# In the last two blocks VectorE instead of ScalarE makes every second high half of the turned probabilities

## The chip, the cores and the metric

The kernel runs on one core of one Trainium2 chip. The metric is the device time of one execution in microseconds (us); shorter is better. Before the change it is 729.9 us, the median of 3 runs (729.87 to 730.22).

## The reference, cut to what matters

The layer that this case touches is an attention over a graph with 4096 nodes: scores, a mask by the adjacency matrix, a softmax along each row, and the weighted mean of `value`.

```python
def _L1_gnn_ref(x, neigh, adj, ...):
    neib_att = jnp.tanh(neigh @ Wn1 + bn1) @ Wn2 + bn2
    value = neigh @ Wv + bv
    x_att = jnp.tanh(x @ Wx1 + bx1) @ Wx2 + bx2
    ws = jnp.einsum('nh,mh->nm', x_att, neib_att)
    ws = jax.nn.leaky_relu(ws, negative_slope=0.01)
    ws = jnp.where(adj > 0, ws, jnp.float32(NEG_BIG))
    ws = jax.nn.softmax(ws, axis=1)
    agg_neib = ws @ value
    return jnp.concatenate([x @ Wfx + bfx, agg_neib], axis=1)
x = _layernorm(x + _L0_gnn_ref(x, adj, ...))
x = _layernorm(x + _L1_gnn_ref(x, neigh, adj, ...))
```

`_L0_gnn_ref` averages the neighbours' rows (mask @ x over the degree) and mixes them with the node's own row through small weight matrices.

## The kernel before, in words

The 4096 rows are worked on in 32 blocks of 128 rows (b = 0 to 31). Along the 4096 neighbours a block has 8 chunks of 512 columns. All engines walk through the same numbered slots s; `due(s, at)` gives the block and the chunk whose turn it is, so that chunk k of a step with the offset `at` comes up in slot 8b + k + at. Several blocks are in work at the same time: in slot 8b + 23 + k the scores of chunk k are made (`SCORE_AT`), in slot 8b + 31 the row maximum (`ROW_MAX_AT`), then four exponentials of 1024 columns in the order quarter 1, 0, 2, 3 in the slots 8b + 32, 33, 34 and 36 (`EXPS`). The order within a slot is that of each engine's loop over s, and every engine works strictly in that order; semaphores carry the dependences.

The probabilities must stand transposed for the product with `value`. The first quarter (two chunks) goes over DMA: ScalarE rounds it to a high half (`wide_high`, L925), VectorE makes the low half, the rest that the rounding left (`wide_low`, L761), SyncE issues the DMA transposes (L376). The other six chunks are turned by TensorE; they are counted j = 0 to 5 here, and n = 6b + j over all blocks. One of them goes like this:

- TensorE transposes it into one of two PSUM buffers `ps_t[n % 2]` (`turn_p`, L1116, slot 8b + 33 + j). It waits for the exponential, and for the low half of turn n - 2.
- ScalarE copies it as f16 to `p_hi[:, n % 2]` (`p_high`, L920). It waits for the turn and, for the buffer, until weighing n - 2 has finished.
- VectorE subtracts: `p_lo = ps_t - p_hi` (`p_low`, L756). It waits for `p_hi_made`.
- TensorE multiplies both halves with the values (`weigh_values`, L1137, one slot later, 12 matmuls). It waits for the low half. The first weighing of a block also waits until VectorE has read the sums of the block before (`layer1`, L773).

In the slots in which block b's chunks are turned, block b + 1's scores are made: TensorE `scores` (L1107, two PSUM buffers), ScalarE `leaky` (L907), VectorE `masked_scores` (L692), and after its eighth chunk VectorE's `row_max` (L698, L701), which lets the exponentials (L913) of block b + 1 start. Block 31 has no block after it. Within a slot VectorE's order is `layer1`, `masked_scores`, `row_max`, `wide_low`, `p_low`; ScalarE's is `exps`, `wide_high`, `p_high`, `leaky`, `normalise2` (L937); TensorE's is `turn_p`, `scores`, `weigh_values`. GpSimd's `norm2` (L473 to L477) stands between `layer1` and `normalise2`, and the store of a block follows that.

Of the kernel before, what the change touches and what calls it, by code (L numbers as in the profile page):

```python
# [18 lines left out]
NB = N // P  # L19
# [5 lines left out]
NG = N // GW  # L25
# [22 lines left out]
NT = NB // TR  # L48
MASK_BUFS = 4
RES_BUFS = 4  # L50

# [18 lines left out]
TURN_AT = 33  # L72
# [6 lines left out]
BY_PE = NG - 2 * BY_DMA  # L79
# [16 lines left out]
def due(s, at, k=None):  # L96

    b, g = divmod(s - at, NG)
    return (b, g) if 0 <= b < NB and (k is None or g == k) else None
# [8 lines left out]
def turned_by_pe(s, at):  # L108

    d = due(s, at)  # L110
    return (*d, d[0] * BY_PE + d[1]) if d and d[1] < BY_PE else None


def at_least(eng, sem, value):
    if value > 0:
        eng.wait_ge(sem, value)


def gnn_kernel(nc, x, adj, w_self, b_self, w_nb, b_nb, w_comb, b_comb, neigh, wx1, bx1, wx2, bx2,
# [5 lines left out]
    with ExitStack() as ctx:  # L125
# [3 lines left out]
        def sem(name):  # L129
            return ctx.enter_context(nc.semaphore(name))  # L130
# [38 lines left out]
        p_hi, p_lo = p_both[:, 0], p_both[:, 1]  # L169
        res = late[:, 1024:2048].rearrange("p (r d) -> p r d", r=RES_BUFS)  # L170

# [53 lines left out]
        ps_t = [ctx.enter_context(nc.psum_tensor(f"ps_t{k}", [P, GW], F32)) for k in range(2)]  # L225
# [54 lines left out]
        pt_done = sem("pt_done")  # L280
        pv_done = sem("pv_done")
# [22 lines left out]
        m_split = sem("m_split")  # L304
        m_scaled = sem("m_scaled")
        p_hi_made = sem("p_hi_made")
        wide_hi_made = [sem(f"wide_hi_made{w}") for w in range(BY_DMA)]
        wide_lo_made = [sem(f"wide_lo_made{w}") for w in range(BY_DMA)]
        wide_t_in = [sem(f"wide_t_in{w}") for w in range(BY_DMA)]
# [119 lines left out]
        def _(pool):  # L429
# [35 lines left out]
            def add_biases(b):  # L465
                pool.wait_ge(x1_made, b + 1)
                at_least(pool, out_made, b - RES_BUFS + 1)
                pool.tensor_tensor(res[:, b % RES_BUFS, :], x1[:, :], bfv_sb[:, :], ALU.add).then_inc(resx_made, 1)  # L468

# [18 lines left out]
        def _(dve):  # L488
# [260 lines left out]
            def add_fx(b):  # L749
                dve.wait_ge(resx_made, b + 1)  # L750
                dve.scalar_tensor_tensor(out=res[:, b % RES_BUFS, 0:DV], in0=ps_x[:, 3 * P:4 * P], scalar=fx_inv,
                                         in1=res[:, b % RES_BUFS, 0:DV], op0=ALU.mult, op1=ALU.add).then_inc(res_made, 1)

            def p_low(b, j, n):
                dve.wait_ge(p_hi_made, n + 1)
                dve.tensor_tensor(p_lo[:, n % 2, :], ps_t[n % 2][:, :], p_hi[:, n % 2, :],  # L756
                                  ALU.subtract).then_inc(p_lo_made, 1)

# [5 lines left out]
            def layer1(b):  # L764
                base = 5 * b
                right = res[:, b % RES_BUFS, DV:D]
                dve.wait_ge(pv_done, NG * (b + 1))
# [44 lines left out]
        def _(act):  # L812
# [61 lines left out]
            def first_part(s):  # L874
                if s == 0:
                    n_high(PRE - 1)
                if (t := turn_due(s, 0)) is not None:
                    if t + 1 < NT:
                        copy_rows_t(t + 1)
                    v_high(t)  # L880
                if (t := turn_due(s, 1)) is not None:
                    hidden(t)
                if (t := turn_due(s, 2)) is not None:
                    n_high(t)
                if s + 2 < NT:
                    x_high(s + 2)
                if s in (6, 7):
                    act.wait_ge(m_scaled, 1)
                    act.activation(m16[:, 0, s - 6, :], m_both[:, s - 6, :], ACT.Copy, scale=m_scale).then_inc(m_hi_made, 1)

            def mean_of(b):
                act.wait_ge(degree_step, 2 * (b + 1))
                at_least(act, mean_t_done, b)
                act.activation(mean[:, :], ps_agg[b % 2][:, 0:D], ACT.Copy, scale=row[:, 5:6]).then_inc(mean_made, 1)

            def mean_high(b):
                act.wait_ge(mean_t_done, b + 1)
                at_least(act, combined, b)
                act.activation(mean_t[:, 0, :], ps_agg[b % 2][:, 0:D], ACT.Copy, scale=x_scale).then_inc(mean_hi_made, 1)

            def leaky(b, k):
                act.wait_ge(s_done, NG * b + k + 1)
                if k < 2 * BY_DMA:
                    at_least(act, wide_lo_made[k // 2], b - 1)
                else:
                    at_least(act, pt_done, BY_PE * (b - 2) + k - 2 * BY_DMA + 1)
                act.activation(score[:, b % 2, k * GW:(k + 1) * GW], ps_s[k % 2][:, :], ACT.Prelu, alpha=SLOPE,  # L907
                               scale=score_scale).then_inc(leaky_made, 1)

            def exps(b, q):  # L910
                act.wait_ge(max_step, 2 * (b + 1))
                part = score[:, b % 2, q * QW:(q + 1) * QW]
                act.activation(part, part, ACT.Exp, bias=exp_bias[:, b % 2:b % 2 + 1],  # L913
                               scale=score_unit).then_inc(exp_made, 1)

            def p_high(b, j, n):
                act.wait_ge(pt_done, n + 1)

                at_least(act, pv_done, NG * b + j - 1 if j >= 2 else NG * (b - 1) + BY_PE + j - 1)
                act.copy(p_hi[:, n % 2, :], ps_t[n % 2][:, :]).then_inc(p_hi_made, 1)  # L920

            def wide_high(b, w):
                act.wait_ge(exp_made, NQ * b + EXP_PLACE[w] + 1)
                at_least(act, wide_t_in[w], 32 * b)
                act.copy(wide_p[:, w, 0, :], score[:, b % 2, w * QW:(w + 1) * QW]).then_inc(wide_hi_made[w], 1)  # L925

            def normalise1(b):
                act.wait_ge(norm1_step, 3 * (b + 1))
                at_least(act, x1_t_done, b)
                at_least(act, resx_made, b)  # L930
                act.activation(x1[:, :], l0[:, :], ACT.Identity, scale=mv1[:, 3:4],  # L931
                               bias=mv1[:, 4:5]).then_inc(x1_made, 1)

            def normalise2(b):
                act.wait_ge(norm2_step, 3 * (b + 1))
                at_least(act, out_sent[b % 2], 16 * (b // 2))
                act.activation(out_sb[:, b % 2, :], res[:, b % RES_BUFS, :], ACT.Identity, scale=mv2[:, 3:4],  # L937
                               bias=mv2[:, 4:5]).then_inc(out_made, 1)

            def x1_high(b):  # L940
                act.wait_ge(x1_t_done, b + 1)
                at_least(act, hf_done, b)
                act.activation(x1_t[:, 0, :], ps_x[:, 0:D], ACT.Copy, scale=X1_SCALE).then_inc(x1_hi_made, 1)

            def x_tanh(b):
                act.wait_ge(hf_done, b + 1)
                at_least(act, xatt_done, b)
                at_least(act, tanh_split, b)
                for out in (tanh32, tanh16):
                    act.activation(out[:, :], ps_x[0:H3, 2 * P:3 * P], ACT.Tanh, bias=bx1_sb[0:H3, 0:1],  # L950
                                   scale=h1_inv[0:H3, :]).then_inc(tanh_made, 1)

            def xatt_high(b):
                act.wait_ge(xatt_done, b + 1)
                at_least(act, s_done, NG * (b - 1))
                act.activation(stack[:, b % 2, :], ps_x[0:H3, 0:P], ACT.Identity,
                               bias=bx2_sb[0:H3, 0:1]).then_inc(xatt_hi, 1)

            for s in range(0, SLOTS + 3):
                first_part(s)  # L960
                if d := due(s, MEAN_SPLIT_AT, 0):
                    mean_high(d[0])
                if d := due(s, X1_AT, 0):
                    normalise1(d[0])
                if d := due(s, X1_COPY_AT, 0):
                    x1_high(d[0])
                if d := due(s, TANH_AT, 0):
                    x_tanh(d[0])
                if d := due(s, STACK_AT, 0):
                    xatt_high(d[0])  # L970
                for at, q in EXPS:
                    if d := due(s, ROW_MAX_AT + 1 + at, 0):
                        exps(d[0], q)
                for w, at in enumerate(WIDE_HIGH_AT):
                    if d := due(s, at, 0):
                        wide_high(d[0], w)
                if d := turned_by_pe(s, TURN_AT):
                    p_high(*d)
                if d := due(s, SCORE_AT):
                    leaky(*d)  # L980
                if d := due(s, MEAN_AT, 0):
                    mean_of(d[0])
                if d := due(s, LAYER1_AT + 1, 0):
                    normalise2(d[0])
# [248 lines left out]
```

## Time and profile before

| | before |
|---|---|
| median of 3 runs | 729.9 us (729.87 to 730.22) |
| the profiled execution, its own time | 730.62 us |
| its span in the profile | 728.8 us |
| TensorE (PE) busy | 689.6 us, 95% |
| VectorE (DVE) busy | 621.7 us, 85% |
| ScalarE (ACT) busy | 573.5 us, 79% |
| GpSimd (POOL) busy | 129.9 us, 18% |

The shares are means over the whole span. The change touches only the last two blocks, whose turns lie in the last 35 us or so, and there the shares are others; so the trace has to be read by stretch and in order of time. Times in the rows are counted from the start of the span.

### The profile page before, as it was taken

The numbers are of one execution on the slowest core, as the hardware profiler recorded it, in microseconds if no ns is written. First come the engines' busy times: TensorE is split into PE (matmuls) and PEld (weight loads), VectorE is DVE, ScalarE is ACT, GpSimd is POOL, SyncE is SP. The second block draws the span as 40 slices with busy tenths as digits, with TensorE's granted clock in tenths as the row PEclk, the third lists the DMA queues.
The fourth block names the chain that finished last, engine by engine and source line by source line (L and its number), as shares of the span: only waits on it lengthen the run. The fifth ranks groups of instructions, "written<-read, shape, count | busy, mean of one in ns | idle before, by whom it ended". The sixth has DMA issues, their size and how long they took to land.

```text
span 728.8 us, 19763 instructions
## 1 busy us (share of the span) xinstructions
PE 689.6 (95%) x7344; PEld 592.1 (81%) x7344; DVE 621.7 (85%) x1535; ACT 573.5 (79%) x920; POOL 129.9 (18%) x242
## 2 busy tenths in 40 slices
PE   5989998999999999999999999999999999998775
PEld 4646676888888888888888888888888888886554
DVE  4887668999999999999999999999999999987874
ACT  2455248888888888888888888888888888889884
POOL 0010111222211222221111222211122221111101
PEclk9989999999999999999999999999999999999999
DMA  8967999999999999999999999999999999841111
GB/s 266 370 150 165 228 269 236 195 203 223 196 202 206 223 208 202 216 224 213 220 212 208 208 203 219 188 221 205 206 200 217 212 220 217 167 81 33 39 42 44
DMA packets 260145, 141.39 MB, mean 194 GB/s; under 512 B 225361, under 2 KB 243665, under 8 KB 260049
## 3 DMA queue, kind: packets, MB, share of 16 engines
q1 hardware_dynamic: 259604, 140.10, 88.7%
q8 instruction: 59, 0.97, 0.6%
q14 instruction: 38, 0.30, 0.1%
q10 hardware_dynamic: 444, 0.02, 0.0%
HBM read 81.35 MB, written 4.19 MB: 117 GB/s over the span
## 4 chain that ended last, share of the span: by engine, by line
PE 86%; ACT 5%; DVE 4%; issue 3%; POOL 1%; DMA 1%; SPq 0%; POOLq 0%; ACTq 0%
PE ps_v L1137 22%; PE ps_agg L1092 15%; PE ps_agg L1095 14%; PE ps_t L1116 10%; PE ps_s L1107 7%; PE ps_agg L1156 3%; PE ps_agg L1159 3%; PE ps_s L1006 2%; PE ps_v L1014 2%; PE ps_x L1176 1%; PE ps_x L1179 1%; ACT score L913 1%; PE ps_t L997 1%; PE ps_x L1023 1%; DMA neigh_sb<-in_L_gnn_neigh_dram 1%
## 5 line engine op out<-in xcount | busy, mean ns | idle before, releaser
L1092 PE MATMUL ps_agg<-x,mask_t 128*128 128x257 f16 x1024 | 243.4, 274 | 0.2 <-DMA mask_t<-mask 0.2
L1095 PE MATMUL ps_agg<-x,mask_t 128*128 128x256 f16 x1024 | 237.4, 273 | 0.3 <-DVE x L533 0.3
L907 ACT ACTIVATE score<-ps_s,sc 128x512 f32<-128x512 f32 x256 | 178.7, 698 | 63.1 <-PE ps_s L1107 57.6
L692 DVE CUSTOM_DVE_ANT_0 score<-score,mask 128x512 f32<-128x512 f32 x256 | 175.9, 687 | 16.7 <-ACT score L907 14.3
L1137 PEld LDWEIGHTS ps_v<-v,late 128*128 128x128 f16 x2304 | 143.9, 97 | 41.7 <-DVE late L756 16.9
L1137 PE MATMUL ps_v<-v,late 128*128 128x129 f16 (+1 forms) x2304 | 162.6, 219 | 11.6 <-DVE late L773 6.0
L913 ACT ACTIVATE score<-score,exp_bias,sc 128x1024 f32<-128x1024 f32 x128 | 159.4, 1246 | 3.2 <-DVE exp_bias L701 3.2
L756 DVE TENSOR_TENSOR late<-ps_t,late 128x512 f16<-128x512 f32 x192 | 130.7, 681 | 33.2 <-ACT late L920 31.4
L920 ACT CAST late<-ps_t 128x512 f16<-128x512 f32 x192 | 114.8, 598 | 20.4 <-PE ps_t L1116 20.4
L1116 PE MATMUL ps_t<-ident,score 128*128 128x128 f32 x768 | 116.8, 275 | 5.3 <-ACT score L913 5.1
L1095 PEld LDWEIGHTS ps_agg<-x,mask_t 128*128 128x128 fp8e4 x1024 | 100.3, 98 | 15.5 <-issue 5.2
L1092 PEld LDWEIGHTS ps_agg<-x,mask_t 128*128 128x128 fp8e4 x1024 | 100.5, 98 | 15.1 <-issue 0.8
L1107 PE MATMUL ps_s<-n,stack 96*128 96x512 f16 x256 | 97.3, 380 | 1.0 <-DVE stack L746 0.9
L544 DVE TENSOR_SCALAR mask<-adj_sb 128x1024 bf16<-128x1024 int32 x128 | 89.8, 704 | 3.9
L1116 PEld LDWEIGHTS ps_t<-ident,score 128*128 128x128 f32 x768 | 80.9, 141 | 7.3 <-ACT score L913 7.1
L473 POOL TENSOR_SCALAR mv<-mv 128x1 f32<-128x1 f32 x32 | 18.9, 590 | 232.9 <-DVE mv L779 232.9
L1137 PEld LDWEIGHTS ps_v<-v,neigh_sb 128*128 128x128 f16 x768 | 49.0, 97 | 7.9
L1137 PE MATMUL ps_v<-v,neigh_sb 128*128 128x129 f16 (+1 forms) x768 | 54.0, 219 | 0.0
L459 POOL TENSOR_SCALAR mv<-mv 128x1 f32<-128x1 f32 x32 | 7.9, 246 | 248.9 <-DVE mv L730 248.9
L761 DVE TENSOR_TENSOR neigh_sb<-score,neigh_sb 128x1024 f16<-128x1024 f32 x32 | 39.2, 1224 | 0.9
L468 POOL TENSOR_TENSOR late<-x,bfv_sb 128x256 f32<-128x256 f32 x32 | 27.8, 868 | 45.1 <-ACT x L931 45.1
L925 ACT CAST neigh_sb<-score 128x1024 f16<-128x1024 f32 x32 | 34.8, 1087 | 0.0
(133 smaller groups left out, 805.4 us busy)
## 6 DMA issues: line engine op xcount, KB each, us to landing
adj_sb<-in_adj_dram SPq DMA_DIRECT2D x128, 512.0 KB, 5.3
neigh_sb<-in_L_gnn_neigh_dram SPq DMA_DIRECT2D x8, 512.0 KB, 8.0
score<-in_x_dram SPq DMA_DIRECT2D x8, 512.0 KB, 8.5
x_in<-in_x_dram SPq DMA_DIRECT2D x32, 128.0 KB, 2.7
out_dram<-out_sb SPq DMA_DIRECT2D x32, 128.0 KB, 3.3
mask_t<-mask SPq DMA_TRANSPOSE x128, 4.8
neigh_sb<-neigh_sb SPq DMA_TRANSPOSE x64, 3.7
mask<-in_L_gnn_W_comb_dram SPq DMA_DIRECT2D x1, 512.0 KB, 9.2
```

What stands on the lines that cost most here:

```text
L544: dve.tensor_scalar(mask[:, b % MASK_BUFS, q * QW:(q + 1) * QW], adj_sb[:, q, :], 0.0, EDGE, ALU.is_le, ALU.add).then_inc(mask_made, 1)
L692: dve.tensor_tensor_reduce(score[:, b % 2, part], score[:, b % 2, part], mask[:, b % MASK_BUFS, part], 1.0, -3.0e38, ALU.subtract, ALU.max ...
L756: dve.tensor_tensor(p_lo[:, n % 2, :], ps_t[n % 2][:, :], p_hi[:, n % 2, :], ALU.subtract).then_inc(p_lo_made, 1)
L761: dve.tensor_tensor(wide_p[:, w, 1, :], score[:, b % 2, w * QW:(w + 1) * QW], wide_p[:, w, 0, :], ALU.subtract).then_inc(wide_lo_made[w], 1)
L907: act.activation(score[:, b % 2, k * GW:(k + 1) * GW], ps_s[k % 2][:, :], ACT.Prelu, alpha=SLOPE, scale=score_scale).then_inc(leaky_made, 1)
L913: act.activation(part, part, ACT.Exp, bias=exp_bias[:, b % 2:b % 2 + 1], scale=score_unit).then_inc(exp_made, 1)
L920: act.copy(p_hi[:, n % 2, :], ps_t[n % 2][:, :]).then_inc(p_hi_made, 1)
L1092: mm = pe.matmul(agg[:, 0:D + 1], mask_t8[:, c, 0, :], x16[:, c, X_HI:X_ONE + 1], start=(c == 0), stop=(c == NC - 1), skip_group_check=True)
L1095: mm = pe.matmul(agg[:, 0:D], mask_t8[:, c, 0, :], x16[:, c, X_LO:X_LO + D], start=False, stop=False, skip_group_check=True)
L1107: pe.matmul(ps_s[k % 2][:, :], stack[:, b % 2, :], n16[:, k * GW:(k + 1) * GW], start=True, stop=True).then_inc(s_done, 1)
L1116: mm = pe.transpose(ps_t[n % 2][:, u * P:(u + 1) * P], score[:, b % 2, at:at + P], ident[:, :])
L1137: mm = pe.matmul(ps_v[:, 0:n], p, v16[:, c, v:v + n], start=(j == 0 and u == 0 and part == 0), stop=(j == NG - 1 and u == CG - 1 and part ...
```

## The change

For blocks 30 and 31 and j = 1, 3 and 5, six chunks in all, ScalarE leaves `p_high` out. VectorE makes the high half at the place of its low half: it waits for the turn (`pt_done`) and for the buffer (`pv_done`), copies `ps_t` to `p_hi` with the same tile shapes and types, waits for its own copy, and then subtracts as before. The waits on `p_hi_made` of all other chunks count only the copies that ScalarE makes. Nothing else changes place.

```diff
--- before.py
+++ after.py
@@ -48,6 +48,7 @@
 NT = NB // TR
 MASK_BUFS = 4
 RES_BUFS = 4
+LAST = 2
 
 
 
@@ -109,6 +110,16 @@
 
     d = due(s, at)
     return (*d, d[0] * BY_PE + d[1]) if d and d[1] < BY_PE else None
+
+
+def high_by_dve(b, j):
+
+    return b >= NB - LAST and j % 2 == 1
+
+
+def highs_by_act(b, j):
+
+    return sum(not high_by_dve(*divmod(i, BY_PE)) for i in range(b * BY_PE + j + 1))
 
 
 def at_least(eng, sem, value):
@@ -304,6 +315,7 @@
         m_split = sem("m_split")
         m_scaled = sem("m_scaled")
         p_hi_made = sem("p_hi_made")
+        late_hi_made = sem("late_hi_made")
         wide_hi_made = [sem(f"wide_hi_made{w}") for w in range(BY_DMA)]
         wide_lo_made = [sem(f"wide_lo_made{w}") for w in range(BY_DMA)]
         wide_t_in = [sem(f"wide_t_in{w}") for w in range(BY_DMA)]
@@ -752,7 +764,13 @@
                                          in1=res[:, b % RES_BUFS, 0:DV], op0=ALU.mult, op1=ALU.add).then_inc(res_made, 1)
 
             def p_low(b, j, n):
-                dve.wait_ge(p_hi_made, n + 1)
+                if high_by_dve(b, j):
+                    dve.wait_ge(pt_done, n + 1)
+                    at_least(dve, pv_done, NG * b + j - 1 if j >= 2 else NG * (b - 1) + BY_PE + j - 1)
+                    dve.tensor_copy(p_hi[:, n % 2, :], ps_t[n % 2][:, :]).then_inc(late_hi_made, 1)
+                    dve.wait_ge(late_hi_made, n + 1 - highs_by_act(b, j))
+                else:
+                    dve.wait_ge(p_hi_made, highs_by_act(b, j))
                 dve.tensor_tensor(p_lo[:, n % 2, :], ps_t[n % 2][:, :], p_hi[:, n % 2, :],
                                   ALU.subtract).then_inc(p_lo_made, 1)
 
@@ -974,7 +992,7 @@
                 for w, at in enumerate(WIDE_HIGH_AT):
                     if d := due(s, at, 0):
                         wide_high(d[0], w)
-                if d := turned_by_pe(s, TURN_AT):
+                if (d := turned_by_pe(s, TURN_AT)) and not high_by_dve(*d[0:2]):
                     p_high(*d)
                 if d := due(s, SCORE_AT):
                     leaky(*d)
```

## Rows read from the trace of the kernel before

**Rows 1.** Busy time by stretch: stretch, each engine's busy time (instructions), clock, DMA share, GB/s.

```profile
560.00:600.00 40.00, 40.00 (x454) 35.62 (x452) 36.35 (x95) 33.90 (x56) 8.37 (x15) 1.00 1.00 207
...
694.00:709.00 15.00, 11.12 (x135) 8.81 (x134) 11.76 (x31) 13.23 (x20) 1.70 (x3) 1.00 0.20 46
709.00:728.80 19.80, 10.38 (x140) 8.86 (x137) 7.76 (x17) 9.85 (x13) 2.12 (x6) 0.96 0.16 41
```

**Rows 2.** VectorE in order of time, turns 1 to 5: start, us, line, operation [idle before].

```profile
700.18 0.69 DVE L756 TENSOR_TENSOR late<-ps_t,late 128x512 f16<-128x512 f32 x1
...
701.75 0.69 DVE L756 TENSOR_TENSOR late<-ps_t,late 128x512 f16<-128x512 f32 x1 [0.28 <-ACT late L920]
...
702.96 1.22 DVE L761 TENSOR_TENSOR neigh_sb<-score,neigh_sb 128x1024 f16<-128x1024 f32 x1
704.43 0.69 DVE L756 TENSOR_TENSOR late<-ps_t,late 128x512 f16<-128x512 f32 x1 [0.24 <-ACT late L920]
...
707.13 0.69 DVE L756 TENSOR_TENSOR late<-ps_t,late 128x512 f16<-128x512 f32 x1 [0.20 <-ACT late L920]
707.74 0.68 DVE L692 CUSTOM_DVE_ANT_0 score<-score,mask 128x512 f32<-128x512 f32 x1
...
708.46 0.16 DVE L698 TENSOR_REDUCE row<-part_max 128x1 f32<-128x8 f32 x1
708.66 0.21 DVE L701 TENSOR_SCALAR exp_bias<-row,sc 128x1 f32<-128x1 f32 x1
```

**Rows 3.** ScalarE in order of time, same stretch, high halves 1, 2, and last leaky score.

```profile
699.12 0.58 ACT L920 CAST late<-ps_t 128x512 f16<-128x512 f32 x1
...
701.10 0.61 ACT L920 CAST late<-ps_t 128x512 f16<-128x512 f32 x1
...
706.99 0.69 ACT L907 ACTIVATE score<-ps_s,sc 128x512 f32<-128x512 f32 x1
```

**Rows 4.** TensorE in order of time, same stretch: weighing 3, turn 5, last score chunk.

```profile
705.17 0.86 PE L1137 MATMUL ps_v<-v,late 128*128 128x129 f16 x12 [0.33 <-DVE late L756]
705.87 0.61 PE L1116 MATMUL ps_t<-ident,score 128*128 128x128 f32 x4
706.31 0.38 PE L1107 MATMUL ps_s<-n,stack 96*128 96x512 f16 x1
```

**Rows 5.** VectorE in order of time, last block: low halves 1 and 3 to 5.

```profile
713.77 0.66 DVE L756 TENSOR_TENSOR late<-ps_t,late 128x512 f16<-128x512 f32 x1
...
715.87 1.22 DVE L761 TENSOR_TENSOR neigh_sb<-score,neigh_sb 128x1024 f16<-128x1024 f32 x1
717.45 0.69 DVE L756 TENSOR_TENSOR late<-ps_t,late 128x512 f16<-128x512 f32 x1 [0.36 <-ACT late L920]
718.32 0.69 DVE L756 TENSOR_TENSOR late<-ps_t,late 128x512 f16<-128x512 f32 x1 [0.17 <-ACT late L920]
720.16 0.69 DVE L756 TENSOR_TENSOR late<-ps_t,late 128x512 f16<-128x512 f32 x1 [1.15 <-ACT late L920]
```

**Rows 6.** ScalarE in order of time, last block: high half 2, last exponential, high halves 4, 5.

```profile
714.65 0.59 ACT L920 CAST late<-ps_t 128x512 f16<-128x512 f32 x1 [0.34 <-PE ps_t L1116]
...
715.73 1.23 ACT L913 ACTIVATE score<-score,exp_bias,sc 128x1024 f32<-128x1024 f32 x1
...
717.70 0.59 ACT L920 CAST late<-ps_t 128x512 f16<-128x512 f32 x1 [0.28 <-PE ps_t L1116]
719.54 0.59 ACT L920 CAST late<-ps_t 128x512 f16<-128x512 f32 x1 [1.25 <-PE ps_t L1116]
```

**Rows 7.** TensorE in order of time, last block: turn 4, weighing 3, turn 5.

```profile
717.00 0.66 PE L1116 MATMUL ps_t<-ident,score 128*128 128x128 f32 x4
718.20 0.86 PE L1137 MATMUL ps_v<-v,late 128*128 128x129 f16 x12 [0.54 <-DVE late L756]
718.89 0.61 PE L1116 MATMUL ps_t<-ident,score 128*128 128x128 f32 x4
```

**Rows 8.** Groups of VectorE instructions by line and shape: count, busy us, mean ns, idle before.

```profile
L756 DVE TENSOR_TENSOR late<-ps_t,late 128x512 f16<-128x512 f32 x192 | 130.7, 681 | 33.2 <-ACT late L920 31.4
L544 DVE TENSOR_SCALAR mask<-adj_sb 128x1024 bf16<-128x1024 int32 x128 | 89.8, 704 | 3.9
...
L525 DVE SCALAR_TENSOR_TENSOR v<-ps_s,sc,v 128x512 f16<-128x512 f32 x8 | 5.9, 748 | 2.6 <-ACT v L827 2.4
...
L769 DVE RECIPROCAL row<-ps_v 128x1 f32<-128x1 f32 x32 | 5.1, 158 | 2.3 <-PE ps_v L1137 2.3
```

## The prediction

> **What bounds the kernel now.** I read the busy times by stretch first. In the middle of the kernel TensorE has no free moment (40.00 of 40.00 us) [rows 1]. In the last 35 us this is over: from 694 to 709 us, where block 30's chunks are turned, TensorE works 11.1 of 15 us, ScalarE 13.2 and VectorE 11.8; from 709 us on it is 10.4, 9.9 and 7.8 of 19.8 us [rows 1]. Nobody is full there, so the end is set by a chain of waits, and the shares can't say what the change is worth. What can is the three engines' timelines laid beside each other, chunk by chunk.
>
> In block 30's stretch two things are to be seen. VectorE has only three short rests, 0.28, 0.24 and 0.20 us, each in front of a low half and each ended by ScalarE's high half [rows 2]. And what must come out of this stretch is VectorE's row maximum (708.46) and bias (708.66) of block 31 [rows 2], since all exponentials of block 31 wait for it. The low half of chunk 5 (707.13), the last masked score (707.74) and the row maximum follow each other on VectorE almost without a gap [rows 2]. So this stretch belongs to VectorE nearly as much as to ScalarE: whatever is added to VectorE beyond its rests moves block 31.
>
> In block 31's stretch the chain runs: last exponential (715.73), low half 3 (717.45), weighing 3 (718.20), turn 5 (718.89), high half 5 (719.54), low half 5 (720.16), and then the last matmuls, the closing layer norm and the store [rows 5 to 7]. ScalarE waits there for TensorE (0.34, 0.28 and 1.25 us before high halves 2, 4 and 5 [rows 6]).
>
> **The price of one moved copy.** No VectorE copy out of PSUM stands in the trace. The nearest row is the low half itself: it reads the same `ps_t`, writes f16 of the same shape and takes 681 ns [rows 8]. Below it: if the copy ran at two elements per cycle, as the mask's 1024 elements in 704 ns do [rows 8], it would be 158 ns (the PSUM operation with one element [rows 8]) plus half of the mask's remaining 546 ns, 0.43 us. Above it: the two-step operation on 512 PSUM elements, 748 ns [rows 8]. I take 0.68, because the low half shares source, output and length with the copy. Both ends are kept.
>
> The low half must then wait for VectorE's own copy. Such a wait is seen between the row maximum and the bias: 708.46 + 0.16 to 708.66, 0.04 us [rows 2]. An independent instruction, on the other hand, starts about 0.08 us before the one in front has ended (707.13 + 0.69 against 707.74 [rows 2]). So one moved copy delays its low half by s = 0.68 + 0.04 = 0.72 us, counted from when VectorE is free. The two added waits, for the turn and for the buffer, I cost at nothing: in each case the turn and weighing n - 2 are over before VectorE gets there. Behind them are queued the low half and the masked scores of the next chunk.
>
> The Trainium skill, "VectorE: DVE Perf Modes", section "Why PSUM operands drop a tier", says that an fp32 source in PSUM holds VectorE to one element per cycle. Its table of cycles (section on the TRN2 errata) gives 120 + 512 cycles at 0.96 GHz, 0.66 us; by that s would be 0.70 and the sum below 1.5 us instead of 1.6. No row here shows the copy; the low half's 681 ns fits one element per cycle.
>
> **Block 30, step by step.** VectorE's free time before a low half is the rest plus the 0.08 us of overlap: 0.36 before chunk 2, 0.32 before chunk 3, 0.28 before chunk 5 [rows 2].
> - Copy 1: the low half of chunk 1 (700.18) comes 0.72 later. Masked score 3 follows, late by as much; the rest before low half 2 takes 0.36 of it. Left 0.36. Weighing 1 and turn 3 on TensorE come 0.7 later, which still is ahead of their use.
> - Copy 3: wide_low (702.96) is 0.36 late, the rest of 0.32 goes, the copy adds 0.72: low half 3 comes 0.76 late. So do weighing 3 (705.17) and, behind it in TensorE's order, turn 5 (705.87), which ends at 707.24, and score chunk 7 (706.31) [rows 4].
> - Copy 5: VectorE is free at 707.61, 0.76 late, after the turn has ended. The rest of 0.28 goes, the copy adds 0.72: low half 5 comes 1.20 late. The last masked score, the row maximum and the bias come 1.20 late with it.
>
> Sum: 3 x 0.72 - 0.96 = +1.20 us. ScalarE's side: high halves 1, 3 and 5 are gone. High half 2 (701.10) comes 0.47 earlier, since 699.12 to 699.59 is no longer taken [rows 3]. That is worth nothing: VectorE reaches low half 2 later than before anyway. The last leaky score (706.99 before [rows 3]) now waits for score chunk 7, starts at about 707.5 and is over by 708.2, before VectorE wants it at 708.94. So ScalarE's relief is off the path in this stretch.
>
> **Block 31.** All of it starts 1.20 us later; I count in the old times.
> - Copy 1: stands before low half 1 (713.77 [rows 5]), which comes 0.72 later. High half 2 at 714.65 waits for turn 2, which is ahead of weighing 1 in TensorE's order, so it stays. Weighing 1, turn 3 and weighing 2 slip, up to where turn 4 stood anyway (717.00, just behind the last exponential [rows 6, 7]); cost at most 0.05. The last exponential stays at 715.73, because normalise2 ahead of it waits for GpSimd's chain, which starts before copy 1. Cost on the path: nothing.
> - Copy 3: wide_low (715.87 + 1.22 - 0.08) frees VectorE at 717.01. Low half 3 starts at 717.73 instead of 717.45: +0.28. Here 0.44 us of waiting for ScalarE covered the rest of the copy.
> - Weighing 3 and turn 5 come 0.28 later [rows 7]. Low half 4 (718.32) stays, as VectorE is free again at 718.34.
> - Copy 5: ScalarE's high half 5 took from 719.54 to the low half's start at 720.16, 0.62 us [rows 5, 6]; VectorE's takes 0.72. +0.10.
>
> Sum: +0.38 us. Everything behind (last matmuls, layer norm, store) only moves.
>
> **The whole sum** is 1.20 + 0.38 = 1.58 us, or in general 5s - 2.02. The profiled execution took 730.62 us of its own (span 728.8), 0.7 above the median; with 1.58 it would be 732.2. On the median of 729.9 it gives 731.5 us, +0.22%. What a measurement of this kernel can tell from no change is about 0.2%, here 1.46 us. The forecast lies just beyond, so its two sides must share the chance.
>
> **The rivals.**
> - The copy is cheap. At 0.43 us s is 0.47 and the sum 5 x 0.47 - 2.02 = +0.33 us: 730.2 us, no change to be measured. The total is negative only if the copy is shorter than 0.36 us (s below 0.404). For it: one input and one output. Against it: the low half's rate, one element per cycle from PSUM [rows 8]. The table of tiers on the same page of the Trainium skill allows a copy from any PSUM source up to twice the rate, which is this case; its rule for fp32 sources is the other. No row decides.
> - ScalarE's relief is worth more than I count. This ends on the faster side. ScalarE is the busiest engine from 694 to 709 us [rows 1], and three casts of 0.47 to 0.6 us leave it in each block. If VectorE's rests are all that stood between the kernel and a gain, they are 0.96 us in block 30 and about 0.4 before low half 3 of block 31: at most 1.4 us less, 728.5 us, from the point at which the added copies hide elsewhere. Against it: they can't, since VectorE takes them in order, right ahead of the row maximum.
> - VectorE pays more per chunk. With 0.75 us for the copy, s = 0.79 and the sum is +1.93: 731.8 us. If each of the added waits also took 0.04 to 0.08 us, five times up to 0.1, it is 732.3.
> - TensorE's clock falls. Its waits for the low halves grow by up to 0.7 us, and it was granted full speed (1.00) from 694 to 709 us and 0.96 behind [rows 1]. At 1.2 instead of 2.4 GHz weighing 3 (0.69 us to the next start), turn 5 (0.61) and the matmuls behind would take about twice as long: at least 1.3 us more, 732.8 us or above.
> - That the change does nothing is ruled out: both counts of the semaphores are changed with it, and all six copies change engines.
>
> **How the numbers follow.** Forecast, a sum of 1.2 to 1.7 us around 731.5: 0.64, of which 0.39 above the bound of 731.36 and 0.25 below. Cheap copy, 730.2: 0.15. Relief, down to 728.5: 0.05, of which 0.03 faster beyond the bound. VectorE pays more: 0.12. Clock: 0.04. So faster 0.03, same 0.25 + 0.15 + 0.02 = 0.42, slower 0.39 + 0.12 + 0.04 = 0.55. The range goes from just under the cheap copy's 730.2 to 732.3; it leaves out the clock and most of the relief, and a part of the others.
>
> **What would show it.** The changed profile should have six VectorE casts of about 0.68 us and six casts fewer on ScalarE; VectorE without a rest from about 700.2 us to the bias, which comes at about 709.9 instead of 708.66; ScalarE waiting longer, for that bias and for turns; in block 31, VectorE's rest before low half 3 gone, and the distance from the bias to the last low half longer by 0.4 us. A bias at its old time would mean that the copy is cheap or that rests elsewhere took it; a low half 5 of block 31 that comes sooner after the bias would mean that ScalarE's relief counts. The clock must stay at 1.00 until the last matmul.

## The result

The changed kernel takes 731.71 us (median of 22 runs, 730.83 to 732.96) against 730.21 us (22 runs, 729.26 to 731.44). The ratio is 1.0021, with a 95% interval of 1.0015 to 1.0028: 0.21% slower, about +1.5 us. The forecast was 731.5 us, +0.22%, with 0.55 on slower.

| | before | after |
|---|---|---|
| the profiled execution, its own time | 730.62 | 731.69 us |
| its span | 728.8 | 729.9 us |
| VectorE busy | 621.7 | 625.1 us |
| ScalarE busy | 573.5 | 570.8 us |
| masked score 1 of block 30's stretch to the bias of block 31 | 12.72 | 13.90 us |
| bias of block 31 to the closing reciprocal | 14.50 | 14.88 us |

The last two lines are differences of starting times in the traces (before: 695.94 to 708.66 to 723.16). They are the sound measure here: the two profiled executions enter the stretch 0.48 us apart (695.94 and 695.46), although up to there both kernels do the same work in the same order. Together they have grown by 1.18 + 0.38 = 1.56 us, the measured difference.

First the price, in the groups of VectorE instructions by shape (columns as in rows 8):

```profile
L774 DVE TENSOR_TENSOR late<-ps_t,late 128x512 f16<-128x512 f32 x192 | 130.5, 680 | 30.3 <-ACT late L938 28.3
...
L770 DVE CAST late<-ps_t 128x512 f16<-128x512 f32 x6 | 4.1, 682 | 0.8 <-PE ps_t L1134 0.8
```

Six casts of 682 ns stand there, two nanoseconds from the low half beside them. VectorE in order of time, from masked score 1 to the bias of block 31 (columns as in rows 2, with what comes ahead of turn 1):

```profile
695.46 0.69 DVE L704 CUSTOM_DVE_ANT_0 score<-score,mask 128x512 f32<-128x512 f32 x1 [1.28 <-ACT score L925]
...
699.70 0.68 DVE L770 CAST late<-ps_t 128x512 f16<-128x512 f32 x1
700.42 0.69 DVE L774 TENSOR_TENSOR late<-ps_t,late 128x512 f16<-128x512 f32 x1
...
701.63 0.68 DVE L774 TENSOR_TENSOR late<-ps_t,late 128x512 f16<-128x512 f32 x1
...
702.84 1.22 DVE L779 TENSOR_TENSOR neigh_sb<-score,neigh_sb 128x1024 f16<-128x1024 f32 x1
703.98 0.68 DVE L770 CAST late<-ps_t 128x512 f16<-128x512 f32 x1
704.70 0.69 DVE L774 TENSOR_TENSOR late<-ps_t,late 128x512 f16<-128x512 f32 x1
...
705.91 0.69 DVE L774 TENSOR_TENSOR late<-ps_t,late 128x512 f16<-128x512 f32 x1
...
707.12 0.68 DVE L770 CAST late<-ps_t 128x512 f16<-128x512 f32 x1
707.84 0.69 DVE L774 TENSOR_TENSOR late<-ps_t,late 128x512 f16<-128x512 f32 x1
708.45 0.68 DVE L704 CUSTOM_DVE_ANT_0 score<-score,mask 128x512 f32<-128x512 f32 x1
...
709.36 0.21 DVE L713 TENSOR_SCALAR exp_bias<-row,sc 128x1 f32<-128x1 f32 x1
```

Behind low half 0 (697.07 us, after a rest of 0.90 us as before) no bracket with a rest follows up to the bias: all three rests of [rows 2] are gone. A copy is followed by its low half after 0.72 us each time (699.70 to 700.42, 703.98 to 704.70, 707.12 to 707.84). ScalarE and then TensorE in the same stretch (columns as in rows 3 and 4; of TensorE also weighing 3 and turn 5 of the last block, as in rows 7):

```profile
700.15 0.60 ACT L938 CAST late<-ps_t 128x512 f16<-128x512 f32 x1
...
703.84 0.59 ACT L938 CAST late<-ps_t 128x512 f16<-128x512 f32 x1 [0.31 <-PE ps_t L1134]
...
707.00 0.69 ACT L925 ACTIVATE score<-ps_s,sc 128x512 f32<-128x512 f32 x1 [1.98 <-PE ps_s L1125]
```

```profile
705.44 0.85 PE L1155 MATMUL ps_v<-v,late 128*128 128x129 f16 x12 [1.42 <-DVE late L774]
...
719.17 0.86 PE L1155 MATMUL ps_v<-v,late 128*128 128x129 f16 x12 [0.81 <-DVE late L774]
719.87 0.61 PE L1134 MATMUL ps_t<-ident,score 128*128 128x128 f32 x4
```

ScalarE now waits 1.98 us before the last leaky score, where it came straight from high half 5 before; weighing 3 waits 1.42 us for its low half instead of 0.33 [rows 4]. The last block on VectorE (columns as in rows 5; 714.48, 717.71 and 720.51 are the copies):

```profile
714.48 0.67 DVE L770 CAST late<-ps_t 128x512 f16<-128x512 f32 x1
...
716.58 1.21 DVE L779 TENSOR_TENSOR neigh_sb<-score,neigh_sb 128x1024 f16<-128x1024 f32 x1
717.71 0.68 DVE L770 CAST late<-ps_t 128x512 f16<-128x512 f32 x1
718.42 1.29 DVE L774 TENSOR_TENSOR late<-ps_t,late 128x512 f16<-128x512 f32 x2
720.51 0.69 DVE L770 CAST late<-ps_t 128x512 f16<-128x512 f32 x1 [0.80 <-PE ps_t L1134]
721.23 0.69 DVE L774 TENSOR_TENSOR late<-ps_t,late 128x512 f16<-128x512 f32 x1
724.24 0.17 DVE L787 RECIPROCAL row<-ps_v 128x1 f32<-128x1 f32 x1 [2.31 <-PE ps_v L1155]
```

Counted from the bias, low half 3 comes at 718.42 - 709.36 = 9.06 us (8.79 before), low half 5 at 11.87 (11.50 before [rows 2, 5]). The chain that ended last, in order of time (start, us, what), goes through the moved copies in both blocks:

```profile
702.92 1.14 DVE neigh_sb L779
704.06 0.61 DVE late L770
...
707.20 0.61 DVE late L770
...
708.45 0.68 DVE score L704
...
709.36 0.23 DVE exp_bias L713
...
720.51 0.70 DVE late L770
```

The busy times by stretch (columns as in rows 1) show a granted clock of 1.00 up to the bias. Behind it the clock is 1.00 up to the closing reciprocal (724.24) and 0.95 after that, when TensorE has no work left. So no part of the difference is TensorE's clock:

```profile
694.00:709.70 15.70, 10.25 (x129) 8.36 (x126) 13.08 (x33) 11.48 (x17) 1.45 (x3) 1.00 0.22 42
709.70:729.90 20.20, 10.12 (x140) 8.89 (x137) 9.65 (x20) 8.32 (x10) 2.11 (x6) 0.99 0.16 41
```

### The profile page after: what moved, and what is told of

It is laid out like the page before. It is cut to its first block, busy times and chain, and to the rows that moved or that the text cites. A ratio compares the mean times of both kernels' runs of the same rounds, so it can differ in the third digit from the quotient of the medians.

```text
span 729.9 us, 19763 instructions
## 1 busy us (share of the span) xinstructions
PE 688.5 (94%) x7344; PEld 591.8 (81%) x7344; DVE 625.1 (86%) x1541; ACT 570.8 (78%) x914; POOL 129.4 (18%) x242
## 4 chain that ended last, share of the span: by engine, by line
PE 82%; DVE 6%; ACT 4%; issue 4%; DMA 2%; SPq 1%; POOL 1%; POOLq 0%; ACTq 0%; DVEq 0%
PE ps_v L1155 21%; PE ps_agg L1110 14%; PE ps_agg L1113 14%; PE ps_t L1134 10%; PE ps_s L1125 7%; PE ps_agg L1174 3%; PE ps_agg L1177 3%; PE ps_s L1024 2%; PE ps_v L1032 2%; PE ps_x L1194 1%; PE ps_x L1197 1%; PE ps_t L1015 1%; DVE score L704 1%; ACT score L931 1%; PE ps_agg L1165 1%
## 5 line engine op out<-in xcount | busy, mean ns | idle before, releaser
L938 ACT CAST late<-ps_t 128x512 f16<-128x512 f32 x186 | 111.2, 598 | 20.0 <-PE ps_t L1134 20.0
```

## The experiments

Two theories stand against each other. The sum: a moved copy costs the path 0.72 us of VectorE's time less the rests that it fills, and what it saves on ScalarE is worth nothing where VectorE comes later anyway. The relief: ScalarE is the busiest engine of the stretch, so taking casts from it must give something back. Each run gives three lengths from its trace beside the time: bias of block 28 to bias of block 30, masked score 1 to the bias of block 31, and from there to the closing reciprocal. A time carries about 0.5 to 1 us of uncertainty either way, so for small effects the lengths decide; each of them comes from one profiled execution. Lengths are in us, and the sum is that of their changes against the kernel before.

| kernel | bias 28 to 30 | score 1 to bias 31 | bias 31 to end | sum of changes | time, ratio to before (95%) |
|---|---|---|---|---|---|
| before | 35.36 | 12.72 | 14.50 | | |
| the change | 35.36 | 13.90 | 14.88 | +1.56 | 1.0021 (1.0015 to 1.0028) |
| block 30 only | 35.37 | 13.91 | 14.51 | +1.21 | 1.0018 (1.0008 to 1.0027) |
| block 31 only | 35.38 | 12.71 | 14.89 | +0.40 | 1.0008 (1.0000 to 1.0017) |
| copies made twice | 35.39 | 16.09 | 16.87 | +5.77 | 1.0078 (1.0064 to 1.0092) |
| no copy at all | 35.38 | 11.75 | 14.16 | -1.29 | 0.9982 (0.9973 to 0.9991) |
| chunk 1 only | 35.36 | 12.75 | 14.50 | +0.03 | 0.9996 (0.9987 to 1.0005) |
| chunk 0 only | 35.35 | 12.22 | 14.35 | -0.66 | 0.9991 (0.9982 to 0.9999) |
| chunk 0, four blocks | 34.33 | 12.23 | 14.34 | -1.68 | 0.9985 (0.9977 to 0.9994) |
| late normalise2 | 36.20 | 12.38 | 14.17 | +0.17 | 1.0007 (0.9994 to 1.0019) |
| both | 34.34 | 11.89 | 14.00 | -2.35 | 0.9975 (0.9966 to 0.9984) |
| both, normalise2 of four blocks | 33.36 | 11.89 | 14.01 | -3.32 | 0.9965 (0.9952 to 0.9977) |

**One half of the change each.**

```diff
-    return b >= NB - LAST and j % 2 == 1
+    return b == NB - 2 and j % 2 == 1
```

> VectorE makes high halves 1, 3 and 5 of block 30 only. By the sum (a moved copy costs 0.72 us less the rests of VectorE that it fills) this half of the change costs 3 x 0.72 - 0.96 = +1.2 us against the kernel before, and the bias of block 31 comes 1.2 us later after the last score of the stretch's beginning, while block 31 itself keeps its length from bias to last low half (11.50 us). Rival, the relief of ScalarE gives part of it back: less than +0.8 us. Rival, the cost lies mainly in the last block: near 0.

```diff
-    return b >= NB - LAST and j % 2 == 1
+    return b == NB - 1 and j % 2 == 1
```

> VectorE makes high halves 1, 3 and 5 of block 31 only. By the sum +0.38 us against the kernel before: low half 3 comes 0.28 later, low half 5 another 0.10, and from block 31's bias to its last low half 11.9 instead of 11.5 us. Rival, the cost lies mainly in the last block since nothing comes after it: above +1 us. Rival, relief: 0 or less.

Block 30 alone lengthens its stretch by 1.19 us and leaves block 31 alone (+0.01); block 31 alone costs 0.39 us. The two halves are independent and their sum, 1.58 us, is the whole to 0.02 us. The cost does not lie mainly in the last block, where nothing comes after; it lies where VectorE's next duty, the row maximum, is awaited.

**The price doubled.** Each moved copy is made twice, one after the other.

```diff
+                    made = n + 1 - highs_by_act(b, j)
                     dve.tensor_copy(p_hi[:, n % 2, :], ps_t[n % 2][:, :]).then_inc(late_hi_made, 1)
-                    dve.wait_ge(late_hi_made, n + 1 - highs_by_act(b, j))
+                    dve.wait_ge(late_hi_made, 2 * made - 1)
+                    dve.tensor_copy(p_hi[:, n % 2, :], ps_t[n % 2][:, :]).then_inc(late_hi_made, 1)
+                    dve.wait_ge(late_hi_made, 2 * made)
```

> Each of the six moved copies is made twice, the second waiting for the first, so a moved copy costs 1.44 instead of 0.72 us. If VectorE's own time is the price, all three doublings in block 30 show in full, +2.16 us against the changed kernel; in block 31 copy 1 becomes visible too, as wide_low starts late (free at 717.56 instead of 717.01 in the old times), so low half 3 comes 1.55 late and low half 5 2.37: together 3.36 + 2.37 = +5.7 us against the kernel before. Rival, the price is in the waits or in something that a copy's length does not touch: well below +3 us.

Chunk 5 of block 30 on VectorE:

```profile
708.86 0.68 DVE L771 CAST late<-ps_t 128x512 f16<-128x512 f32 x1
709.57 0.69 DVE L773 CAST late<-ps_t 128x512 f16<-128x512 f32 x1
710.30 0.69 DVE L777 TENSOR_TENSOR late<-ps_t,late 128x512 f16<-128x512 f32 x1
```

The lengths grow by 3.37 and 2.37 us (3.36 and 2.37 expected), the time by 0.78%, 5.7 us. Once the rests are full, VectorE's time is paid in full.

**The price taken away.** The high halves of the six chunks are made by nobody, so the low halves are taken against what the buffer still holds; that part of the computation is left out.

```diff
-                    dve.tensor_copy(p_hi[:, n % 2, :], ps_t[n % 2][:, :]).then_inc(late_hi_made, 1)
-                    dve.wait_ge(late_hi_made, n + 1 - highs_by_act(b, j))
```

> The six high halves are made by nobody; the low half is taken against what the buffer still holds, so this part of the computation is left out. It shows ScalarE's relief with no price on VectorE. By the sum (s = 0 in 5s - 2.02) all the rests go: 0.96 us in block 30 and 1.06 in block 31, -2.0 us against the kernel before; the last weighing of the turned chunks would start at 719.84 in the old times, and if the DMA transposes of block 31, issued at 717.12, have not landed by 720.5, part of the last 0.7 us is not seen: -1.3 to -2.0. Rival, ScalarE's casts were hidden anyway: 0 to -0.5. Rival, ScalarE was the true bound of the stretch and relief is worth its casts: -3 us.

Block 30's stretch shrinks by 0.97 us, its three rests (0.96). So the relief of ScalarE is real, but this is all it can bring: the rests, not the casts' 1.4 us. Block 31 shrinks by 0.34 instead of 1.06. TensorE and SyncE's queue show why:

```profile
717.66 1.62 PE L1153 MATMUL ps_v<-v,late 128*128 128x129 f16 x24
719.83 1.54 PE L1153 MATMUL ps_v<-v,neigh_sb 128*128 128x129 f16 x24 [0.55 <-DMA neigh_sb<-neigh_sb]
```

```profile
715.71 2.58 SPq L388 DMA_TRANSPOSE neigh_sb<-neigh_sb  x2
```

The last 24 matmuls need block 31's first quarter, which goes over DMA. The transposes are issued from 715.71 us on, and TensorE waits 0.55 us for them, until 719.83: 4.12 us after the first issue. In the kernel before:

```profile
717.12 2.58 SPq L376 DMA_TRANSPOSE neigh_sb<-neigh_sb  x2
```

```profile
721.60 1.53 PE L1137 MATMUL ps_v<-v,neigh_sb 128*128 128x129 f16 x24
```

Here the same matmuls start 4.48 us after the issue, so only about 0.35 us could be won before this transfer ends last.

**A copy that fits into the rests.** Only j = 1 is moved, in both blocks.

```diff
-    return b >= NB - LAST and j % 2 == 1
+    return b >= NB - LAST and j == 1
```

> Only high half 1 of blocks 30 and 31 is made by VectorE. By the sum this one is free: in block 30 its 0.72 us go into the rests before low halves 2 (0.36) and 3 (0.32) and a little into that before low half 5, in block 31 it lies beside waits. The stretch from low half 0 of block 30 to the bias of block 31 stays 11.1 us, from the bias to the closing reciprocal 14.5 us: 0 to +0.1 us in all. Rival, every moved copy costs its length on the path: +0.7 us in block 30.

The lengths change by +0.03 and 0.00 us. One copy of 0.68 us is free where 0.36 and 0.32 us of free time follow it; a copy has no price of its own.

**A copy where the receiver rests first.** Only j = 0 is moved, in two blocks and then in the last four.

```diff
-    return b >= NB - LAST and j % 2 == 1
+    return b >= NB - LAST and j == 0
```

> High half 0, not 1, 3, 5, of blocks 30 and 31 is made by VectorE. There VectorE rests 0.9 and 2.9 us before the low half, and ScalarE's cast stands behind an exponential. By the same bookkeeping VectorE can copy before ScalarE could: low half 0 of block 30 comes 0.26 us earlier, ScalarE is 0.47 earlier for high halves 2 and 3, on which VectorE waited; the bias of block 31 comes 0.47 us earlier (counted from masked score 1 of the stretch, 12.72 us before), block 31 is 0.16 us shorter: -0.6 us. Rival, VectorE's time is the price wherever the copy stands: +0.3 to +1.2 us.

```profile
694.80 0.69 DVE L704 CUSTOM_DVE_ANT_0 score<-score,mask 128x512 f32<-128x512 f32 x1 [1.28 <-ACT score L925]
...
695.42 0.69 DVE L770 CAST late<-ps_t 128x512 f16<-128x512 f32 x1
696.14 0.69 DVE L774 TENSOR_TENSOR late<-ps_t,late 128x512 f16<-128x512 f32 x1
```

VectorE makes the copy at 695.42, straight behind masked score 1, where it rested 0.90 us before; ScalarE's cast had to stand behind an exponential. The low half comes 1.34 us after masked score 1 instead of 1.60 (695.94 to 697.54 before), 0.26 earlier as expected. The stretch is 0.50 us shorter, block 31 0.15.

```diff
-    return b >= NB - LAST and j % 2 == 1
+    return b >= NB - 4 and j == 0
```

> As the run on chunk 0, in the last four blocks. In the stretches of blocks 28 and 29 ScalarE is busy almost without a gap and VectorE rests 1.54 and 1.18 us before low half 0. Each should gain the cast's 0.47 us too: -1.5 us against the kernel before. Rival, the first-layer chain of block 31 (mean, layer norm, hidden) sets those stretches and the two more blocks give nothing: -0.6 us.

The two blocks more give 1.03 us (35.36 to 34.33), one cast each, as ScalarE is full there. The first-layer chain does not stand in the way.

**What VectorE waited for.** The kernel before, with one ScalarE step later in the order, and the store behind the wide transposes of the next block.

```diff
+LATE_NORM = (NB - 3, NB - 2)
...
-                if d := due(s, LAYER1_AT + 1, 0):
-                    normalise2(d[0])
+                for at in (1, 3):
+                    if (d := due(s, LAYER1_AT + at, 0)) and (at == 3) == (d[0] in LATE_NORM):
+                        normalise2(d[0])
```

> The kernel before, with normalise2 of blocks 29 and 30 two slots later on ScalarE, behind the last exponential and high halves 3 and 4 (and their stores behind the wide transposes). VectorE's rest before low half 3 (0.32 us in block 30, 0.43 in block 31) is due to ScalarE being late with high half 3; by the bookkeeping it goes: -0.32 us to the bias of block 31, and in block 31 -0.34 us, no more, since the DMA transposes land just behind. Together -0.65 us. Rival, these rests are due to something else than ScalarE's order: 0.

The two lengths shrink by 0.34 and 0.33 us (0.32 and 0.34 expected): low half 3 follows wide_low without a rest, in block 30:

```profile
703.03 1.22 DVE L763 TENSOR_TENSOR neigh_sb<-score,neigh_sb 128x1024 f16<-128x1024 f32 x1
704.16 0.68 DVE L758 TENSOR_TENSOR late<-ps_t,late 128x512 f16<-128x512 f32 x1
```

Yet the time shows no gain (1.0007, interval across 1), where about -0.65 us was expected. Two things on record bear on that. The first is in the profiled execution: bias 28 to bias 30 is 0.84 us longer, in a part where this kernel's order is that of the kernel before. TensorE there, by stretch and in order of time, and one line of ScalarE:

```profile
680.00:683.70 3.70, 1.71 (x19) 1.11 (x17) 2.93 (x10) 3.70 (x7) 0.81 (x2) 1.00 0.00 0
683.70:687.40 3.70, 3.66 (x30) 3.37 (x31) 2.52 (x6) 2.78 (x6) 1.15 (x2) 0.54 0.01 2
687.40:691.00 3.60, 2.99 (x37) 2.37 (x35) 3.29 (x6) 3.60 (x7) 0.00 (x0) 1.00 0.31 83
```

```profile
682.18 0.84 PE L1140 MATMUL ps_v<-v,late 128*128 128x129 f16 x12 [1.76 <-DVE late L775]
...
685.48 1.50 PE L1140 MATMUL ps_v<-v,late 128*128 128x129 f16 x12
```

```profile
685.72 0.69 ACT L909 ACTIVATE score<-ps_s,sc 128x512 f32<-128x512 f32 x1 [0.92 <-PE ps_s L1110]
```

From 683.7 to 687.4 us the granted clock was 0.54, near the lower of the two levels, 1.2 GHz, and twelve matmuls of a weighing took 1.50 us instead of 0.84. ScalarE, which is otherwise busy almost without a gap here, waited 0.92 us for the late scores and started this leaky score 28.00 us behind bias 28 instead of 27.16: that is the 0.84 us. Why the clock fell stays open. Ahead of the fall TensorE had worked 1.71 of 3.70 us; at the same place the kernel before had worked 1.68 of 3.70 us (680.8 to 684.5 us) and was granted 1.00 there and in the 3.7 us behind. In the trace of the doubled copies the clock fell too, to 0.50 from 676 to 678 us, and its bias 28 to bias 30 is 35.39 us, 0.03 above the kernel before. So a fall that I gave 0.04 and placed in the changed stretch exists, in other executions and elsewhere, and what it costs depends on who waits for TensorE just then. How often it comes in the timed runs isn't known.

The second thing lies outside the span. The time of an execution is 1.75 to 1.85 us above its span in the 35 executions of the kernel before, and 1.79 to 2.97 us (median 2.20) in the 12 of this kernel. The median of the spans is 727.8 us against 728.2, so part of the gain is there, and is lost behind or ahead of what the trace covers. In the two kernels below, which put the same step off, it reaches 2.41 and 2.72 us; with chunk 0 in four blocks alone it stays at 1.76 to 1.85. What takes this time is not shown; the store that is put off together with normalise2 was not tried by itself.

**Both together,** as the experiments pointed to a version that beats both kernels: only j = 0 is moved, in the last four blocks, and `LATE_NORM` is as in the run before.

> Chunk 0's high half on VectorE in the last four blocks and normalise2 of blocks 29 and 30 two slots later, together. If the bookkeeping by rests holds, the gains add up but for VectorE becoming the limit before low half 2: bias of block 28 to bias of block 30 34.3 instead of 35.4 us (as the run with chunk 0 in four blocks), masked score 1 to the bias of block 31 11.9 instead of 12.7 us, bias to the closing reciprocal 14.0 instead of 14.5 us: about -2.3 us, 728.0 us or so, faster by 0.3%. Rival, both take away the same rest: -1.7 us as the run with chunk 0 alone.

The gains add up as worked out: 34.34, 11.89 and 14.00 us, together -2.35 us by the lengths, and the timed runs give 728.15 us against 730.15 (0.9975). By the medians of the spans it is 726.2 against 728.4 us. Block 31's transfer seems to hold the end again, by a tenth: the last matmuls start 0.79 us behind weighing 5, and 0.70 in the kernel before. They start 4.13 us behind the issue of the transposes (715.12 us), as in the run before (716.85 to 720.98 us).

```profile
718.46 0.85 PE L1158 MATMUL ps_v<-v,late 128*128 128x129 f16 x12 [0.72 <-DVE late L776]
719.25 1.54 PE L1158 MATMUL ps_v<-v,neigh_sb 128*128 128x129 f16 x24
```

The last run adds blocks 27 and 28 to `LATE_NORM`:

```diff
-LATE_NORM = (NB - 3, NB - 2)
+LATE_NORM = (NB - 5, NB - 4, NB - 3, NB - 2)
```

> As the run before, but normalise2 of blocks 27 and 28 is two slots later too. In the stretches of blocks 28 and 29 ScalarE itself is full, so putting off one of its steps only changes its order: bias of block 28 to bias of block 30 within 0.3 us of the run before. Rival, the last exponential's start sets these stretches as well: another -0.5 to -1.0 us.

Here my expectation was wrong and the rival right: bias 28 to 30 went from 34.34 to 33.36 us. Putting off a step of a full engine does not only change the order; its last exponential of the block starts earlier (in this trace behind the two tanh),

```profile
666.56 0.74 ACT L927 ACTIVATE score<-ps_s,sc 128x512 f32<-128x512 f32 x1
667.14 0.82 ACT L970 ACTIVATE tanh<-ps_x,bx_sb,sc 96x128 f32<-96x128 f32 x2
667.83 1.27 ACT L933 ACTIVATE score<-score,exp_bias,sc 128x1024 f32<-128x1024 f32 x1
```

and everybody who waits for it goes on earlier. Each of the two stretches is 0.49 us shorter (18.47 to 17.98 and 15.87 to 15.38 us), as much as normalise2 holds ScalarE. Where the step is hidden now is only partly seen: ScalarE's rests of 0.22 us before high half 5 of blocks 28 and 29 are gone, and the 0.94 us before the last first-layer norm are 0.78. The time is 727.44 us against 730.15, 0.9965 (0.9952 to 0.9977): by the ratio 2.6 us faster than the kernel before, where the change as made is 1.5 us slower. The lengths give -3.32 us and the medians of the spans -3.35 (725.05 against 728.4 us); the difference lies outside the span, where this kernel's executions have 1.80 to 2.72 us and those of the kernel before 1.75 to 1.86.

## Why the prediction was right, point by point

- **What bounds the stretch.** Right. Block 30's stretch belongs to VectorE once its rests are full; the bias of block 31, 709.36 + 0.48 = 709.84 in the old times, was forecast at 709.9.
- **The price.** 682 ns measured for 0.68 taken from the low half, and 0.04 us for the wait on its own copy: from a copy's start to its low half it is 0.72 us in block 30 and 0.70 to 0.72 in block 31. The Trainium skill, "VectorE: DVE Perf Modes", section "Why PSUM operands drop a tier", has one element per cycle for fp32 from PSUM; the 682 ns, as much as the low half takes, agree with it. The table of cycles on the same page of the Trainium skill, in its section on the TRN2 errata, gives an estimate of 658 ns, 24 ns too few, and the measurement decides.
- **Block 30:** 1.20 forecast, 1.18 in the change's own trace, 1.19 alone. The steps hold too: low half 1 0.72, low half 2 0.36, low half 3 0.75, low half 5 1.19 us later (700.42, 701.63, 704.70, 707.84, each + 0.48, against [rows 2]; 0.72, 0.36, 0.76 and 1.20 forecast). The last leaky score started at 707.48 in the old times, 707.5 forecast.
- **Block 31:** 0.38 forecast, 0.38 and 0.39 measured; low half 3 +0.27, low half 5 +0.37.
- **Edits costed at nothing.** The two added waits cost nothing that can be seen: five of the six copies start where an independent instruction would. The reason given, that the turn is always over before VectorE gets there, does not hold for the sixth: VectorE rests 0.80 us before copy 5 of block 31, until turn 5 has ended. The sum had counted that copy from the turn's end all the same, so nothing was lost by it. Copy 1 of block 31 was free. ScalarE's relief was worth nothing beside the copies, as the rests were filled by them; without copies it is worth 0.97 us in block 30.
- **The rivals.** A cheap copy fell with the 682 ns, and so did the rival in which VectorE pays more. Relief, bounded at 1.4 us, was 1.3 us when the copies are taken away altogether, so the bound was good, though for block 31 by luck: I had not seen the DMA transposes 0.35 us behind the chain, and the 0.4 that I allowed is what they leave. The general form 5s - 2.02 would have given -2.0 at s = 0; it holds only above, where the transfer is hidden. That the formula's lower end was wrong had no weight in the forecast. The clock did not fall before the last matmul in the changed kernel's profiled execution.

What was luck: the forecast lay 0.1 us beyond the bound between slower and no change, and the two sides shared the chance almost evenly. The measured interval, 1.0015 to 1.0028, has that bound of 0.2% inside it. What was not luck is the sum: 1.58 us forecast, 1.56 by the lengths, with each half in its place. The lengths in the traces are good to a few hundredths, but a timed run isn't.

## What to carry to other kernels

When work is moved to another engine, walk along the receiver's timeline: each moved piece costs its length plus the wait on its own result (0.68 + 0.04 us here), less the rests that come behind it before the next thing somebody waits for, and it gains only where it can start before the giver could have made it. So the same 0.68 us copy cost 1.2 us for three in one place, nothing in another, and gave 0.5 us at chunk 0, where the receiver rested first. Look for the step that causes the rests: putting off a step whose result nobody on the path awaits, as normalise2, gained as much by the lengths as a moved chunk 0 (0.67 and 0.66 us in the last two blocks) and gives no engine more work, though alone it did not show in the time. And have an eye on the transfer that lies just behind the chain, which caps the gain in the last block.

## What the runs showed of the hardware that was not expected

- The two DMA transposes of 128 x 1024 f16 halves let TensorE go on 4.12 or 4.13 us after the first was issued, in four traces (715.71 to 719.83 us without the copies, 716.85 to 720.98 with the late normalise2, 715.12 to 719.25 and 713.64 to 717.77 in the last two kernels). The first of these shows TensorE waiting for them; in the others that is inferred from the equal distance. They were 0.35 us from the path in the kernel before.
- TensorE's granted clock fell to 0.54 for some 4 us in one profiled execution (683.7 to 687.4 us) and cost 0.84 us there. The work ahead of it, 1.71 us in 3.70 us, was the same as in the kernel before (1.68 us), which was granted 1.00. In another execution it fell to 0.50 for 2 us (676 to 678 us), where it cost 0.03 us at most.
- In the three kernels that put off normalise2 and its store, an execution's time is up to 2.97 us above its span; in the kernel before it is 1.75 to 1.86 us. The cause is open.
- A VectorE instruction that waits for the result of the one in front starts 0.04 us after its end, an independent one 0.08 us before: here a dependence costs 0.12 us even within an engine.
